# Two blocks of TensorE work change places in each step of a local-attention stack (outputs' products behind the turned queries and keys)

## The reference, cut to what matters

```python
def attn_layer(x, Wqkv, qs, ksc, Wo):
    q, k, v = split(x @ Wqkv)                     # 16 heads of 64
    q = rotate(l2norm(q) * qs); k = rotate(l2norm(k) * ksc)
    sim = einsum('bhwie,bhwje->bhwij', bq, bk2) * 8.0      # "scores"
    attn = softmax(where(mask, -max, sim))
    out = einsum('bhwij,bhwje->bhwie', attn, bv2)          # "outputs"
    return out @ Wo
for i in range(6):
    x = attn_layer(shift_tokens(x), Wqkv[i], ...) + x
    x = ffn_layer(shift_tokens(x), ...) + x
x = x + attention_16_heads(layernorm(x));  x = x + stack(layernorm(x))
x = x + attention_1_head(layernorm(x));    x = x + stack(layernorm(x))
x = x + attention_16_heads(...); x = x + mixture_of_experts(...)
x = x + binarised_attention(...); x = x + mixture_of_experts(...)
```

## Time and profile before

| what | value |
|---|---|
| median of 3 runs | 4307.7 us |
| the profiled execution, its own time | 4315.31 us |
| its span | 4313.5 us |
| instructions | 165583 |
| TensorE products busy | 3889.5 us, 90% |
| GpSimd busy | 3002.4 us, 70% |
| VectorE busy | 2743.1 us, 64% |
| ScalarE busy | 2678.2 us, 62% |
| granted TensorE clock, mean | 0.957 |

### The profile page before, as it was taken

One profiled execution on the slowest core, in us unless ns is written; L12 is line 12 of the kernel. 1 busy time (PEld: TensorE's weight loads), 2 busy tenths in 40 slices (PEclk: granted clock), 3 DMA queues, 4 the chain that ended last, 5 costly groups with the idle time before them and its releaser, 6 DMA issues.

```text
span 4313.5 us, 165583 instructions
## 1 busy us (share of the span) xinstructions
PE 3889.5 (90%) x69444; PEld 2741.9 (64%) x69444; DVE 2743.1 (64%) x4939; ACT 2678.2 (62%) x5554; POOL 3002.4 (70%) x1858
## 2 busy tenths in 40 slices
PE   7989999999999999977999999999999998375976
PEld 4556666766666767645666676767676765153645
DVE  5666766667676767645766666767676765624741
ACT  5657666676766767644666676767666675133752
POOL 0088888888888888825888888888888885611011
PEclk9999999999999999989999999999999999677987
DMA  2033433433334334312334343333433432040004
GB/s 69 2 83 92 110 97 96 111 93 104 104 93 108 99 102 105 91 54 53 95 101 105 89 112 95 102 106 94 109 99 95 111 93 57 0 114 19 2 13 128
DMA packets 349777, 367.29 MB, mean 85 GB/s; under 512 B 58737, under 2 KB 285298, under 8 KB 348786
## 3 DMA queue, kind: packets, MB, share of 16 engines
q1 hardware_dynamic: 338834, 348.59, 30.9%
q0 software_dynamic: 2048, 4.20, 0.3%
q10 hardware_dynamic: 8160, 3.93, 0.3%
HBM read 246.79 MB, written 109.71 MB: 83 GB/s over the span
## 4 chain that ended last, share of the span: by engine, by line
PE 39%; DVE 4%; ACT 3%; issue 3%; POOL 2%; DMA 1%; POOLq 0%; DVEq 0%; ACTq 0%
PE banks L333 6%; PE banks L361 4%; PE banks L374 4%; PE banks L421 3%; PE banks L462 3%; PE banks L317 3%; PE banks L300 2%; PE banks L406 2%; PE banks L391 2%; PE banks L456 1%; PE banks L1457 1%; ACT arena L1071 1%; PE banks L1477 1%; DVE arena L621 1%; PE banks L998 1%
## 5 line engine op out<-in xcount | busy, mean ns | idle before, releaser
L692 POOL TENSOR_TENSOR arena<-arena 128x512 f32<-128x512 f32 x768 | 959.5, 1270 | 394.0 <-DVE arena L621 253.6
L697 POOL TENSOR_TENSOR arena<-arena 128x1024 f32<-128x1024 f32 x384 | 905.9, 2359 | 30.1
L694 POOL TENSOR_TENSOR arena<-arena 128x1024 f32<-128x1024 f32 x384 | 908.1, 2365 | 0.0
L621 DVE SCALAR_TENSOR_TENSOR arena<-arena,banks 128x512 f32<-128x512 f32 x768 | 493.7, 684 | 508.7 <-ACT arena L504 502.1
L333 PE MATMUL banks<-w_qk,arena 128*128 128x512 f32 x1536 | 736.0, 602 | 16.4 <-DVE arena L797 10.6
L472 ACT COPY arena<-banks 128x512 f32<-128x512 f32 x384 | 224.5, 585 | 645.4 <-PE banks L421 645.2
L614 DVE TENSOR_REDUCE arena<-arena 128x8 f32<-128x512 f32 x768 | 487.6, 671 | 83.6 <-ACT arena L488 83.5
L488 ACT ACTIVATE arena<-banks 128x512 f32<-128x512 f32 x768 | 441.4, 593 | 66.3 <-PE banks L333 52.6
L333 PEld LDWEIGHTS banks<-w_qk,arena 128*128 128x128 f32 x1536 | 276.9, 193 | 272.5 <-issue 272.5
L421 PE MATMUL banks<-ident,arena 128*128 128x128 f32 x3072 | 423.1, 281 | 19.4 <-POOL arena L697 19.3
L588 DVE TENSOR_REDUCE arena<-banks 128x8 f32<-128x512 f32 x384 | 264.2, 688 | 212.6 <-PE banks L317 211.6
(11 more groups left out here) (240 smaller groups left out, 6511.2 us busy)
## 6 DMA issues: line engine op xcount, KB each, us to landing
v_rows<-arena SPq DMA_DIRECT2D x1536, 64.0 KB
arena<-v_rows SPq DMA_DIRECT2D x768, 128.0 KB, 2.6
arena<-v_rows SPq DMA_DIRECT2D x768, 112.0 KB, 2.4
arena<-in_moe_w SPq DMA_DIRECT2D x30, 515.5 KB, 3.8
w_qk<-in_stack_qk SPq DMA_DIRECT2D x48, 256.0 KB, 3.0
w_v<-in_stack_v SPq DMA_DIRECT2D x48, 128.0 KB, 3.4
w_o<-in_stack_o SPq DMA_DIRECT2D x12, 512.0 KB
w_w<-in_stack_w SPq DMA_DIRECT2D x12, 341.0 KB, 3.1
```

Of the source, the lines that this page charges most:

```text
L621: last = nc.vector.scalar_tensor_tensor(qn[:, :, tile], rn, 1e12, bank(M, tile).rearrange("p (h q d) -> p h q d", h=GH, q=2), ALU.min, ALU ...
L692: nc.gpsimd.tensor_tensor(f.sined[:, :, :, half, :], x[:, :, :, 1 - half, :], sines[:, :, mine].unsqueeze(1).to_broadcast([D, GH, 4, DH // ...
L694: nc.gpsimd.tensor_tensor(rot, x.rearrange("p h t a d -> p h t (a d)"), cosines.unsqueeze(1).to_broadcast([D, GH, 4, DH]), ALU.mult).then_ ...
L697: nc.gpsimd.tensor_tensor(rot, rot, f.sined.rearrange("p h t a d -> p h t (a d)"), ALU.add).then_inc(S.rotated, 1)
```

## The change

In `pe_stack_step` the call of the two halves of `pe_stack_heads` moves ahead of the block of the outputs. Nothing is added or removed; no other engine's program is touched.

```diff
@@ -302,6 +302,9 @@
                                      f.k[r, u % 2, hp, 32 * win:32 * win + KW], start=False, stop=True,
                                      skip_group_check=True)
         last.then_inc(S.scores, 1)
+    if st.on(2):
+        pe_stack_heads(M, st, 0)
+        pe_stack_heads(M, st, 1)
     if st.on(4):
         u = s - 4
         st.wait(S.probs_taken, u + 1)
@@ -317,9 +320,6 @@
                     last = pe.matmul(bank(M, 4 + par)[c:c + 32, o:o + DH], f.pt[r, win // 4, hp, c:c + 32],
                                      f.vb[r, u % 2, win, hp, :], start=True, stop=True)
         last.then_inc(S.outs, 1)
-    if st.on(2):
-        pe_stack_heads(M, st, 0)
-        pe_stack_heads(M, st, 1)
     pe_stack_hidden(M, st, 0)
     if st.on(0):
         u, g = s, s % G
```

## The result

| what | before | after |
|---|---|---|
| median of 5 runs | 4307.7 us | 4481.99 us (4479.91 to 4486.49) |
| ratio | | 1.0406, 95% interval 1.0391 to 1.0422 |
| the profiled execution, its own time and span | 4315.31, 4313.5 us | 4481.64, 4479.1 us |
| granted TensorE clock, mean | 0.957 | 0.961 |

The changed kernel is 174 us slower. The forecast was +121 (4429), and its range ended at 4480, 2 us short of the result. The direction and most of the waits were right; something was left out.

A forecast was written before the change was run, and what follows sets the result against it. TensorE's order was taken to set the time in the two stacks. Waits of 105.6 + 42.3 + 6, together +154, less 33 us of stops gave +121: 4307.7 to 4429 us, range 4365 to 4480.

The forecast's parts named there:

- No work is added, so the change is worth what it moves: TensorE's step: heads start 0.79 us earlier, outputs 0.92 later, and queries and keys L333 still start at 2.46.
- Step 4: Product L433 waits for ScalarE's copy L548, whose chain follows the later outputs: +0.92 us in each of 46 pairs.
- Step 7: Turned outputs L391 wait for VectorE's L598 and start at 4.70 instead of 4.18: +0.52 us a pair.
- Step 3: VectorE's L588 starts at 2.92 instead of 2.39, so turned outputs L391 wait for L598: +0.53 us a pair.
- Step 6: Heads wait until 1.45 for GpSimd's L697, with ScalarE's late L536 ending at the same 1.4: +0.70 us a pair.
- Step 2: Heads wait for GpSimd's L697 and start at 0.98: +0.24 us a pair.
- The first steps of a layer: GpSimd is late there already; heads lose the rest of their cover, some 0.5 us more each over 12 layers: +6 us.
- The stops: TensorE's 55.4 us of idle without releaser inside outputs L317, taken as instruction fetch: some 45 shorter, 33 counted as gain.
- A: Rival: L536 and L697 come early enough for the heads, only steps 3, 4, 7 pay: +46, 4354 us; chance 0.1.
- B: Rival: same waits, but the idle times without releaser in L317 give nothing back: +154, 4462 us; chance 0.13.
- C: Rival: stops shrink, slack behind VectorE's L588 at L433 and L391 absorbs the rest: -33 to -45, 4268 us; chance 0.05.
- D: Rival: GpSimd's and ScalarE's lateness passes on through later steps, another 1 us a pair: +169, 4477 us; chance 0.09.

## Why the prediction was right and wrong

**The step that failed: "No work is added, so the change is worth what it moves", with L333 "still starts at 2.46".** It starts at 2.58 and lasts 0.1 longer. Behind that sentence stood the sum of durations, 0.92 for the heads and 0.79 for the outputs, as if they did not depend on their neighbours. They do: the kernel before goes from small to full products once a step and ahead of L333 only with transposes, the changed one goes small, full, small, full. The price is 0.02 + 0.10 + 0.10, 0.22 in step 0, where nothing waits. Four kernels with full products between the small ones have it, from 0.18 to 0.31 (with two turns), the number of transposes does not matter (7.17 with one and with four), and the kernel with the outputs ahead of the scores, which has a new order and no turn more, does not have it. The rows before showed one such turn in each step, inside the 0.79 and the 0.92, and nothing from which a second could be priced, so it should have stood in the sum with bounds of its own; it had none, and the range was too narrow on that side.

**The waits, term by term.** The sum was 3.12 a pair and came out at 4.32. Of the 1.20 more, some 0.96 is that price, added up over the steps below (0.22, 0.07, 0.20, 0.08, 0.10, 0, 0.17 and 0.12 for steps 0 to 7): 46 us of the program. Without it the time would have been 4436, 7 from the forecast. The next largest part is a start after a wait: behind ScalarE's copy L536 TensorE starts 0.14 after its releaser, not 0.06 as read from L437, which is 0.08 in each of steps 1, 3 and 6. Behind L598 and GpSimd's L697 it starts 0.05 to 0.06 after, as read.
- Step 4, forecast 0.92, measured 1.02: 0.92 and 0.10 of the turn. The chain was right, as the kernel with ScalarE's copies ahead shows.
- Step 7, 0.52 against 0.70: L391 starts at 4.83 instead of 4.70, since the turn makes the outputs end 0.12 later than forecast, and its four products take 0.49 instead of 0.44 behind the wait. Right mechanism. Step 3, 0.53 against 0.69: L588 starts at 3.07 instead of 2.92, 0.08 of it from the heads' later start and the rest from the turn.
- Step 6, 0.70 against 1.05: the heads start at 1.62 instead of 1.45, because the copy L536 comes at 1.48 and is the later of the two hands, where I had GpSimd's 1.39, and the start after it takes 0.14; the turn, 0.17, is the rest. The sentence on "a second hand" had it, at 1.4.
- Step 1, 0.21 against 0.36: heads at 1.12 instead of 1.04, and 0.07 of the turn.
- Step 2, 0.24 against 0.28, is near by luck. Since step 1 grew by 0.36 and not by 0.21, GpSimd's L697 ends at 0.78 of the median step 2 and the heads start at 0.83, not at 0.98. The wait is 0.08 instead of 0.24, and the turn's 0.20 fills the place. L421 waits for GpSimd 12 times in the steps 2, and the rest of that wait is shorter than the profile counts.
- Step 5, 0 as forecast: the heads wait 0.40 and L437 waits for L551 all the same, 7.5 us in all instead of 18.5.
- Step 0, 0 forecast, 0.22 measured: the bare price.
- The first steps of a layer, +6: misread. The 19.3 us of waits for GpSimd before are 12 waits in the first ten steps of the two stacks, and not one in each of twelve layers. They are 25.9 us after, by my count 2.2 of it in later layers; the sum below leaves 2 us of the span for all of it.

**The stops.** They fell from 55.4 to 6.6, 49 where I had 45. What they cost the steps is less, and the trace tells it when each step with a stop is laid beside the median step of its kind (my count, not a row of a view): 47.7 us before, 11.7 after, so 36 came back where I had 33. Of the difference 11 lies in step 5 before, where 17.4 us of stops make the steps only 6.5 longer, because L437's wait covers the rest. The mechanism was right as well. Step 7 shows it alone, since its heads do not wait. With none, one, four and eight transposes ahead of them the outputs start at 0.76, 1.03, 1.36 and 1.79 of the step, and its stops are 20.5 us in 16, 14.5 in 15, 10.7 in 15 and 3.3 in 11. On average a stop is 0.31, 0.57 and 0.98 shorter where the outputs start 0.27, 0.60 and 1.03 later: it gives back the time that is put ahead of it. In all steps the stops are 55.4, 23.4, 16.7 and 6.6; that the first transpose, of 0.26, brings 32 of the 49 is because in steps 2 and 5 the outputs now stand behind its wait too (0.40 in step 5). Crossing a block is "mostly hidden" by the Trainium skill (Runtime: NRT & Kernel Launch, Instruction fetch mechanics). By their number the trace agrees, 56 stops for 555 packets, but what is not hidden is 55.4 us in the kernel before and 184.7 in the one with the outputs ahead.

**The sum.** 48 x 3.30 for steps 0, 1, 2, 3, 6, 7 is 158 and 46 x 1.02 for step 4 is 47, together 205; less 36 for the stops it is 169. In the traces the time from a stack's first scores to its last grew by 87.0 and 83.9 us, 171 in all; the rest of the program is 5 shorter, which makes the span's 165.6. The forecast was 105.6 + 42.3 + 6 - 33 = 121. The difference of 53 to the medians' 174 is the 1.20 a pair, 58, less 3 of the stops and 4 of the starts; 2 are left over.

**The rivals.** A (the heads do not wait) fell: 105.5 us of waits at L421. B (the stops stay) fell with 6.6. C (faster) fell on the chain that it named, L588 to L433 and L391. D, the delays feeding on through the steps, gave nearly the measured time (4477) by luck: of its 1 us a pair the steps show 0.09, in step 6, where L536 comes behind GpSimd, and most of the rest of what was missing is the turn.

## What to carry to other kernels

Moving a block in an engine's program is not only worth its duration. Read what stands on either side of it in both places: here full products put between groups of small ones cost 0.13 to 0.22 us each time, with one, four or eight of them. Then ask which wait the block had covered (0.77 of cover less turned L536's nothing into 79.6 us), and which engine starts when the block that it is moved past ends (here VectorE's L588, 1.05 later in step 4, which pays it almost in full because a product ends that chain). Where two releasers hold one instruction, taking the later one away is worth only its lead over the other.

## What the runs showed of the hardware

- A single transpose between products on 64 x 32 tiles costs 0.15 us more than one in a row of them (0.26 from start to start, against 0.115 in a row of eight). A full load behind small products, or behind a wait, is not ahead of its product (0.00 instead of 0.11 us), and the products that follow take 0.1 longer (1.99 for 1.88 in L333, 1.13 for 1.02 in L437).
- TensorE starts 0.05 to 0.06 us behind the end of L551, L598 and L697, and 0.14 behind ScalarE's copies L536 and L548.
- A stop without a releaser stands at one place in each block of 256 of TensorE's instructions, and is 1 us on average (55.4 us in 56). Most of these places pass without one (56 of 556). Where something is put ahead of the dense stretch, the stop is shorter by as much (0.98 us for 1.03). The sum of the stops more than triples (55.4 to 184.7 and 181.9 us) where a wait heads the dense stretch. Why, no run here shows.
- Behind many of its stops, which are 1.8 us on average (184.7 us in 100), the granted clock of TensorE fell to 0.50 for a short stretch and came back to 1.00, in the kernel with the outputs ahead of the scores, 41 times in the two stacks.
- Within the stack the profiled executions repeat their steps to some 0.01 us (the kernel before and the one with 24 waits more have the same medians in all eight steps), so a table of step lengths tells a price of 0.1 us where the time of the program only tells 8.
